# Reordering a sixteen-batch transformer-block kernel on all engines, with other places for the last batch's gate products and the first batch's loads

## What is computed

```python
def cross_attention(query, keys, values):            # 16 heads of 32, 120 keys per batch
    Q, K, V = query @ W_q.T, keys @ W_k.T, values @ W_v.T      # split into heads
    scores = Q K^T / sqrt(32) - slope[head] * (query_pos - key_pos)
    scores = where(mask == 0, -inf, scores)
    e = exp(scores - max(scores))
    return (e / (1 + sum(e))) V @ W_o.T
def ffn(x):                                          # x_prev: x moved by one token
    xr, xk = mu_r * x + (1 - mu_r) * x_prev, mu_k * x + (1 - mu_k) * x_prev
    return sigmoid(xr @ W_r.T) * (relu(xk @ W_k.T) ** 2 @ W_v.T)
x = x + tanh(g_xattn) * cross_attention(layernorm(x), ctx, ctx)
x = x + tanh(g_ffn) * ffn(layernorm(x))
```

## Time and profile before

| | before |
|---|---|
| median of 3 runs | 1311.96 us (1311.15 to 1312.66) |
| the profiled execution's own time | 1310.22 us |
| its span, first to last instruction | 1308.4 us |
| mean granted PE clock | 0.998 |
| busy PE / DVE / ACT / POOL | 1282.4 / 1068.7 / 837.4 / 786.9 us |
| mean DMA | 79 GB/s |

### The profile page before, as it was taken

How to read it: one execution, slowest core, us unless ns; L and a number is a source line. 1 busy time by engine, 2 the same in 40 slices (tenths; PEclk the granted TensorE clock), 3 DMA queues, 4 the chain that set the end, 5 groups by cost and what they waited for, 6 DMA issues and landing times.

```text
span 1308.4 us, 30826 instructions
## 1 busy us (share of the span) xinstructions
PE 1282.4 (98%) x9848; PEld 1044.2 (80%) x9848; DVE 1068.7 (82%) x2834; ACT 837.4 (64%) x2868; POOL 786.9 (60%) x731
## 2 busy tenths in 40 slices
PE   8999999999999999999999999999999999999998
PEld 7888778878777777877777787778778877878877
DVE  4667988888888888888888888888888888888864
ACT  5357483956758394765839486674839577584942
POOL 0015567676666667666666766666676766667641
PEclk9999999999999999999999999999999999999999
DMA  8762304031221304022120502222040412212000
GB/s 286 218 202 80 104 27 136 0 109 52 73 88 36 125 8 140 12 75 86 52 108 8 153 0 85 75 73 88 32 129 0 118 43 73 88 48 74 9 26 33
DMA packets 75377, 103.74 MB, mean 79 GB/s; under 512 B 26960, under 2 KB 33104, under 8 KB 75344
## 3 DMA queue, kind: packets, MB, share of 16 engines
q1 hardware_dynamic: 75344, 103.31, 25.2%
HBM read 78.62 MB, written 24.67 MB: 79 GB/s over the span
## 4 chain that ended last, share of the span: by engine, by line
PE 82%; DVE 6%; DMA 5%; issue 4%; POOL 2%; DVEq 0%; ACT 0%; POOLq 0%; SPq 0%
PE rotating L504 58%; PE score_bank L583 5%; PE probs_bank L677 4%; PE attn_bank L688 4%; PE attn_bank L677 4%; DMA rstd_row<-rstd_scratch 4%; PE score_bank L504 4%; PE score_bank L599 1%; DMA rstd_scratch<-rstd 1%; DVE norm L1221 1%; DVE mix_k L1231 1%; POOL rstd L1452 1%; DVE gated L1248 1%; DVE attn_t L1192 1%; PE probs_bank L599 1%
## 5 line engine op out<-in xcount | busy, mean ns | idle before, releaser
L877 ACT ACTIVATE probs<-probs,neg_max 128x120 f32<-128x120 f32 x1024 | 390.7, 388 | 3.6 <-DVE neg_max L1177 3.5
L1471 POOL TENSOR_TENSOR probs<-probs,recip 128x960 f32<-128x960 f32 x128 | 232.1, 1813 | 162.6 <-DVE recip L1188 162.6
L1173 DVE SCALAR_TENSOR_TENSOR probs<-mask_in,score_bank 128x120 f32<-128x120 f32 x1024 | 213.6, 270 | 27.6 <-PE score_bank L583 26.3
L504 PE MATMUL rotating<-w_proj,attn_t 128*128 128x512 f32 x768 | 192.9, 400 | 7.0 <-DVE attn_t L1192 7.0
L877 ACT ACTIVATION_READ_ACCUMULATOR probs<-probs,neg_max 128x1 f32 x1024 | 197.1, 192 | 0.0
L504 PE MATMUL rotating<-w_gate,mixed_gate 128*128 128x512 f32 x768 | 195.2, 400 | 1.2 <-DVE query_t L1158 1.1
L504 PE MATMUL rotating<-w_value,xt_or_act 128*128 128x512 f32 x720 | 180.8, 400 | 0.0
L504 PE MATMUL rotating<-mixed_key,w_key 128*128 128x512 f32 x720 | 178.7, 397 | 0.0
L504 PE MATMUL rotating<-xt_or_act,w_query 128*128 128x512 f32 x744 | 177.3, 394 | 0.0
L504 PEld LDWEIGHTS rotating<-w_proj,attn_t 128*128 128x128 f32 x768 | 140.8, 188 | 42.8 <-issue 12.5
L1177 DVE TENSOR_REDUCE neg_max<-probs 128x4 f32<-128x480 f32 x256 | 167.2, 653 | 8.8
(11 more groups left out here) (126 smaller groups left out, 2205.9 us busy)
## 6 DMA issues: line engine op xcount, KB each, us to landing
x_again<-in_x_dram SPq DMA_DIRECT2D x64, 256.0 KB, 2.7
xt_raw<-in_x_t_dram SPq DMA_DIRECT2D x16, 1024.0 KB, 8.0
xs<-in_x_dram SPq DMA_DIRECT2D x64, 256.0 KB, 5.4
out_dram<-gated SPq DMA_DIRECT2D x64, 256.0 KB, 2.0
rstd_row<-rstd_scratch SPq DMA_DIRECT2D x16, 256.0 KB, 5.3
value_scratch<-gated SPq DMA_DIRECT2D x16, 240.0 KB, 3.6
mask_in<-in_mask_dram SPq DMA_DIRECT2D x16, 240.0 KB, 2.9
keys_t<-key_scratch SPq DMA_DIRECT2D x16, 240.0 KB, 4.8
```

The source lines that it names most:

```text
L504: mm = pe.matmul(bank, stationary(a, c), moving(b, c), start=(i == 0), stop=(i == MATMULS - 1))
L877: e = act.activation(probs[:, t % 2, head, :], probs[:, t % 2, head, :], ACT.Exp, bias=neg_max[:, t % 2, head:head + 1], accum_out=sums[:, ...
L1173: z = dve.scalar_tensor_tensor(out=probs[:, t % 2, head, :], in0=neg_dist[:, t, :], scalar=SLOPES[head], in1=score_banks[j][:, g * NK:(g + ...
L1471: pool.tensor_tensor(part, part, recip[:, t % 2, heads].unsqueeze(2).to_broadcast((P, H // 2, NK)), ALU.mult)\
```

## The change

All five lists of the batch are put in another order; what each call does stays as it is, but for the splitting of `bias` on DVE into `bias_add` and `bias_max`, so that other work can stand between them. In the last batch, gate 0 and gate 1 are made ahead of `turn2(3)`, with other banks, and in the tail gate 2 and gate 3 stand each behind one half of the key products. On SP, loads and stores of the batch change places, and loads of the first batch (the x tiles for batch 1, weight 5) are issued at other points. `load_x` gets waits of its own, since it now stands ahead of stores whose waits it used to rely on.

```diff
 ATTENTION_AND_FFN = (
     ("gate", 0, -1), ("gate", 1, -1), ("key", 0, -1), ("key", 1, -1), ("key", 2, -1), ("key", 3, -1),
-    ("proj", 0, 0), ("value", 0, -1), ("value", 1, -1), ("proj", 1, 0), ("gate", 2, -1), ("value", 2, -1),
-    ("gate", 3, -1), ("proj", 2, 0), ("value", 3, -1), ("proj", 3, 0),
+    ("proj", 0, 0), ("value", 0, -1), ("value", 1, -1), ("gate", 2, -1), ("proj", 1, 0), ("value", 2, -1),
+    ("proj", 2, 0), ("gate", 3, -1), ("value", 3, -1), ("proj", 3, 0), ("query", 0, 1), ("query", 1, 1),
...
-        tail_bank = {("gate", t): rotating[t % 2] for t in range(QT)}
+        tail_bank = {("gate", t): bank for t, bank in enumerate((rotating[0], attn_bank, rotating[1], rotating[0]))}
...
             def load_x(b, t):
+                if earlier(b, 0, 2 * QT):
+                    sp.wait_ge(out_ready, (b - 2) * QT + t + 1)
...
             load_keys(0)
             load_values(0)
+            load_again(1, 0)
             store_chunk(4)
+            load_again(1, 1)
             for t in range(QT):
                 load_x(0, t)
-            load_weight(5)
...
                     load_xt(b + 1)
-                    load_again(b + 1, 0)
-                    load_again(b + 1, 1)
+                    load_weight(5)
...
                         load_again(b + 1, 0)
-                    for t in range(2):
-                        sp.wait_ge(out_ready, (b - 1) * QT + t + 1)
-                        store_out(b - 1, t)
+                        load_again(b + 1, 1)
+                        load_again(b + 1, 2)
+                    sp.wait_ge(out_ready, (b - 1) * QT + 1)
+                    store_out(b - 1, 0)
...
```

PE (between `turn_probs` 2,3 and the queries), and its tail:

```diff
-                use("proj", 1)
                 turn_probs(b, 2, 0)
                 turn_probs(b, 2, 1)
-                use("gate", 2)
+                use("gate", 2, range(9))
+                use("proj", 1)
                 turn_probs(b, 2, 2)
                 turn_probs(b, 2, 3)
+                use("gate", 2, range(9, MATMULS))
                 use("turn2", 0)
-                use("value", 2)
-                use("turn2", 1)
                 all_attends(2)
                 turn_probs(b, 3, 0)
-                use("gate", 3, range(6))
+                use("value", 2)
+                use("proj", 2)
                 turn_probs(b, 3, 1)
-                use("proj", 2)
+                use("turn2", 1)
                 turn_probs(b, 3, 2)
                 turn_probs(b, 3, 3)
-                use("gate", 3, range(6, MATMULS))
+                use("gate", 3)
                 all_attends(3)
+                use("turn2", 2)
                 use("value", 3)
                 use("proj", 3)
-                use("turn2", 2)
                 if last:
                     pe.wait_ge(read["value"], b * QT)
                     gate(b, 0, range(MATMULS), tail_bank).then_inc(done["gate"], 1)
+                    gate(b, 1, range(MATMULS), tail_bank).then_inc(done["gate"], 1)
                 use("query", 0)
                 use("query", 1)
+                use("query", 2)
                 use("turn2", 3)
-                use("query", 2)
                 use("query", 3)
...
-            pe.wait_ge(read["proj"], NB * QT)
-            tail("gate", 1)
...
-            for t in range(2, QT):
-                pe.wait_ge(read["gate"], f * QT + t - 1)
-                tail("gate", t)
+                if half == 0:
+                    pe.wait_ge(read["proj"], NB * QT)
+                else:
+                    pe.wait_ge(read["gate"], f * QT + 1)
+                tail("gate", 2 + half)
```

DVE (the second half of the batch, as it is after the change) and POOL:

```diff
+                bias(b, 3, 2)
+                bias(b, 3, 3)
+                reciprocals(b, 3, 0)
                 normalise2(b, 0)
...
                 residual(b, 1)
                 statistics2(b, 1)
+                after((distances_to_keys, None))
+                attn_low(b, 2)
+                mix_key(b, 0)
                 normalise2(b, 1)
+                reciprocals(b, 3, 1)
                 feed_forward((finish, 2))
+                residual(b, 2)
+                statistics2(b, 2)
                 after((statistics1, 3))
                 mix_gate(b, 0)
+                normalise2(b, 2)
                 mix_key(b, 1)
                 attn_low(b, 3)
                 mix_gate(b, 1)
                 feed_forward((finish, 3))
                 residual(b, 3)
                 statistics2(b, 3)
+                after((query_out, 0), (query_out, 1))
                 normalise2(b, 3)
...
```

```diff
                 normalise_probs(b, 3, 0)
                 edge(b, 0)
                 difference(b, 0)
+                rstd2_of(b, 1)
+                normalise_probs(b, 3, 1)
+                after((split_x_low, 1), (split_x_low, 2))
                 edge(b, 1)
-                normalise_probs(b, 3, 1)
+                rstd2_of(b, 2)
+                after((rstd1_of, None))
                 difference(b, 1)
-                rstd2_of(b, 2)
+                after((split_x_low, 3))
+                if last:
+                    mix_low(b, 0)
+                    mix_low(b, 1)
                 edge(b, 2)
...
```

More of the change, by code:

```diff
@@ L454, in batch @@
                         load_again(b + 1, 0)
-                    for t in range(2):
-                        sp.wait_ge(out_ready, (b - 1) * QT + t + 1)
-                        store_out(b - 1, t)
+                        load_again(b + 1, 1)
+                        load_again(b + 1, 2)
+                    sp.wait_ge(out_ready, (b - 1) * QT + 1)
+                    store_out(b - 1, 0)
                     if not last:
-                        for t in range(1, QT):
-                            load_again(b + 1, t)
+                        load_x(b + 1, 0)
+                    sp.wait_ge(out_ready, (b - 1) * QT + 2)
+                    store_out(b - 1, 1)
+                    if not last:
+                        load_again(b + 1, 3)
                         sp.wait_ge(scores_biased, (b + 1) * QT * G)
                         load_mask(b + 1)
-                        load_keys(b + 1)
-                        load_x(b + 1, 0)
                         load_x(b + 1, 1)
-                    if not last:
+                        load_x(b + 1, 2)
                         store_rstd(b + 1)
@@ L1160, in query_out, with bias_add @@
                                          op0=ALU.mult, op1=ALU.mult).then_inc(read["query"], 1)
-            def bias(b, t, g):
+            def bias_add(b, t, g):
                 if g == 0:
@@ L1178, in bias @@
                                   AX.X, ALU.max, negate=True).then_inc(max_ready, 1)
+            def bias(b, t, g):
+                bias_add(b, t, g)
+                bias_max(b, t, g)
             def reciprocals(b, t, half):
@@ L1308, in batch @@
                 bias(b, 0, 2)
+                reciprocals(b, 0, 0)
                 bias(b, 0, 3)
-                reciprocals(b, 0, 0)
-                bias(b, 1, 0)
+                after((statistics1, 0))
+                bias_add(b, 1, 0)
+                reciprocals(b, 0, 1)
+                bias_max(b, 1, 0)
                 bias(b, 1, 1)
-                reciprocals(b, 0, 1)
                 bias(b, 1, 2)
@@ L1316, in batch @@
                 reciprocals(b, 1, 0)
+                after((statistics1, 1))
                 bias(b, 2, 0)
-                bias(b, 2, 1)
+                bias_add(b, 2, 1)
                 attn_low(b, 0)
-                bias(b, 2, 2)
+                bias_max(b, 2, 1)
+                bias_add(b, 2, 2)
                 reciprocals(b, 1, 1)
+                bias_max(b, 2, 2)
                 bias(b, 2, 3)
+                after((statistics1, 2))
                 residual(b, 0)
+                bias(b, 3, 0)
                 statistics2(b, 0)
-                after((statistics1, 0))
-                bias(b, 3, 0)
                 bias(b, 3, 1)
@@ L1330, in batch @@
                 attn_low(b, 1)
+                feed_forward((finish, 1))
+                reciprocals(b, 2, 1)
                 bias(b, 3, 2)
+                bias(b, 3, 3)
+                reciprocals(b, 3, 0)
                 normalise2(b, 0)
-                reciprocals(b, 2, 1)
-                feed_forward((finish, 1))
-                reciprocals(b, 3, 0)
                 residual(b, 1)
                 statistics2(b, 1)
-                bias(b, 3, 3)
+                after((distances_to_keys, None))
+                attn_low(b, 2)
+                mix_key(b, 0)
                 normalise2(b, 1)
-                after((statistics1, 1), (statistics1, 2))
+                reciprocals(b, 3, 1)
                 feed_forward((finish, 2))
-                attn_low(b, 2)
-                reciprocals(b, 3, 1)
+                residual(b, 2)
+                statistics2(b, 2)
                 after((statistics1, 3))
-                residual(b, 2)
-                mix_key(b, 0)
-                statistics2(b, 2)
                 mix_gate(b, 0)
+                normalise2(b, 2)
                 mix_key(b, 1)
@@ L1355, in batch @@
```

(3 more changed lines are left out.)

113 lines of the change are left out of this document (61 added, 52 removed).

## The result

| | before | after |
|---|---|---|
| median of the runs | 1312.31 us | 1287.49 us (1286.61 to 1287.98) |
| ratio, 95% interval | | 0.9815 (0.9801 to 0.9829) |
| profiled execution, its span | 1310.22, 1308.4 us | 1286.61, 1284.8 us |
| busy PE / DVE | 1282.4 / 1068.7 us | 1271.9 / 1048.6 us |
| length of a batch | 75.05 us | 73.63 us |

(The median of before is that of the runs made beside it.) The change makes the kernel 24.8 us faster, 1.9%. The forecast was 1292 us, the range 1282 to 1306.

The account below looks back on a forecast made before the run. PE's own work, busy 98%, was taken as the bound. Span 1308.4 - 15.4 (loop) - 0.8 (first batch) - 3.8 (tail) = 1288.4 us; 1290.2 us profiled, 1292 us for the runs; range 1282 to 1306.

Parts of the forecast that it names:

- Loop: Batches after the first: 75.05 us each falling to 73.95 us, 15.4 us gained over 14 batches.
- The walk through the queues: PE's order set out from gate 0 (T = 0), other engines laid beside it, to find new waits; next gate 0 at 73.5.
- two tight places: turn2(2) at T = 56.1 and proj 3 at 59.4, without slack; new waits of 0.2 us a batch for both.
- scores beside attends: Scores 2 directly ahead of attends 0 saves one slow change between kinds of matmul: half of 0.20 us taken, 0.10 a batch.
- part 1: Proj 1 on PE: two groups of transposes and nine gate 2 matmuls in front remove its wait, 0.75 us a batch.
- part 2: turn2(3) behind query 2 on PE, 2.73 us later: its wait goes, 0.29 plus 0.16 us a batch.
- First batch: Wait ahead of turn2(2) may stay in part, query_out 2's is not touched: 0.8 us gained, bounds 0.5 lost and 2.5 gained.
- Tail: Last batch's end: idle ahead of turn2(3) and slow clock go, 1.0 us idle at gate 2 stays; 3.8 us gained, bounds 2 and 4.9.
- SP: Moved loads and stores on SP cost nothing; without cover, a load of 3 to 6 us once per batch.
- R1: POOL's rstd1_of power holds DVE's normalise2(2); turn2(2) waits 1.15 us a batch, 13.3 us less gain, 1305 us; chance 0.14.
- R2: POOL's holds of DVE between attn_low 2 and attn_low 3 delay proj 3: 2.8 us new waits a batch, 1328 us; chance 0.12.

Follow-up runs that it names:

- difference 1 between: Changed kernel with difference 1 between the addition and the power of the 512 scales (rstd1_of) on POOL: 1284.49 us, ratio 0.9802; once more, 1284.21 us.
- difference 1 first: Changed kernel with difference 1 ahead of rstd1_of, the making of the scales, on POOL: 1289.75 us, ratio 0.9839.
- the reduction added: Changed kernel with one unused reduction of 128x512 elements on DVE ahead of the second layer norm of tile 2: 1285.47 us, ratio 0.9809.

## Why the prediction was right, and where it was not

**Loop.** Forecast 73.95 us a batch, measured 73.63; 15.4 us against 19.0 (18.5 and batch 1's 0.5). The walk through the queues held at its two tight places: norm 2 was to end at T = 55.5 and ended at 723.92 - 668.5 = 55.4; attention 3's low part at 59.25 and 59.1. Elsewhere not all of it held: norm 0 ended at 709.85 - 668.5 = 41.4 where I had 41.9, and `attn_low` 2 ended at 46.4 as forecast although its parts did not (the mask came after 0.34 us and not 0.7, and the `distances_to_keys` behind it took 1.71 us where they had taken 0.88 before). New waits were to be 0.2 us a batch and are 0.17. The terms that were too small: scores beside attends, half of 0.20 taken, all of it measured (0.23 in the run that parts them); and one wait of before that I did not count, `turn2(0)`, 0.60 us in the chain of before where 0.44 is four transposes (by the trace it waited for the last `bias` of tile 3, which ended 0.1 us before). These give 0.10 + 0.16 + 0.03 = 0.29 us; part 2 takes 0.06 from it, so that of the 0.32 us some 0.1 stays open.

```profile
721.83 0.60 PE score_bank L599 x4
```

**The step that failed in its reason** is part 1: I gave the 0.75 us at proj 1 to the gate matmuls put in front of it. With these taken away proj 1 does not wait either (0.2 us once in the whole span). The other moves are enough to remove its wait, through `finish` 0, which takes 0.93 us instead of 1.46; which of them does it, on DVE, POOL or PE, was not tested one by one. The gates in front are needed for something that I did not name, ACT's queue of `probs_out` and exponentials; without them the kernel is slower than before (75.83 us a batch). That the size came out was luck in part: the old wait is gone either way, and its size was read from the trace of before; what the move I named is worth, 2.2 us a batch, I had wrong by a factor of three.

**Layer norm of tile 3** (part 2): 0.45 forecast, 0.39 measured on its own. The price of an idle time was too high there: 0.6 us for 0.45, not 0.7.

**First batch.** 0.8 us forecast, within bounds of 0.5 lost and 2.5 gained; measured 0. The 1.2 us ahead of `turn2(2)` went, but the wait for `query_out` 2 grew from 1.10 to 2.46 us: I had said that it was not touched. It is counted from the end of the queries, and these now end earlier, while the split of weight 5 took 3.12 us where it had taken 2.27 in the trace of before. `query_out` 2 starts at 151.12 in both.

```profile
146.13 2.27 DVE L1117 TENSOR_TENSOR w_value<-xs,w_value 128x2048 fp32r<-128x2048 f32 x1
```

```profile
145.85 3.12 DVE L1132 TENSOR_TENSOR w_value<-xs,w_value 128x2048 fp32r<-128x2048 f32 x1
```

**Tail.** 3.8 us forecast, 4.55 in the traces, 4.1 by the undone tail. Gate 2 waited 0.73 us where I had 1.0, and a key half takes 1266.96 - 1261.20 = 5.76 us where I had 5.9; the values begin 1269.70 - 1245.88 = 23.8 us after proj 3 and not 24.7. No lower clock, as forecast.

**SP.** I took its moves at nothing. No run undoes them; PE waits for no DMA in any of these traces, and in the changed kernel's batch `query_out` 0 waits for PE (0.83 us) and no longer for the scales' load (0.45 us before).

**Rivals.** R1 falls for the power and holds for a full-size operation; in the changed kernel only the small one stands beside that norm. R2 (holds that add up between `attn_low` 2 and 3) did not occur: there was one hold of 0.87 us (`finish` 2, 1.62 us), and norm 2 behind it ended on time all the same. A rival that I did not have, a wait on ACT, was the one that decides here whether proj 1 may stand in front.

## What to carry to other kernels

With one engine 98% busy, an order can still be worth 2%: set its work out by the pitch of its pieces, lay the other queues beside it and compare at each wait; that walk was good to 0.2 us here at the two places without slack, and up to 0.5 us off elsewhere. Give a removed wait to an edit only after undoing that edit alone, since a move on one engine may be there for a queue on another. Operations of full size that hold each other, here norms, `finish` and splits on DVE against differences, scalings and low parts on POOL, should not become ready at the same time; a small operation ahead of the large one settles who goes first.

## What the runs showed of the hardware that I had not expected

Between kernels that do the same at the end of the first batch, PE idled 2.46 to 2.54 us there, and its granted clock fell behind it in some traces and not in others. It stayed at 1.00 in both traces of the changed kernel (2.46 and 2.50), the one with proj 1 back (2.46), the one with scores and attends apart (2.52) and the first of the one with difference 1 between (2.54); it fell in the one with difference 1 first (2.52; two stretches of 2 us):

```profile
152.00:154.00 2.00, 2.00 (x10) 1.17 (x13) 2.00 (x4) 0.00 (x0) 1.73 (x2) 0.73 1.00 332
154.00:156.00 2.00, 2.00 (x33) 1.79 (x30) 1.81 (x7) 1.26 (x3) 0.09 (x1) 0.50 0.97 330
```

From gate 0 to the same piece of the next batch it then took 229.88 - 151.78 = 78.10 us instead of 76.89, 1.0 us more beside the 0.17 of its longer batch. It also fell with the old tail (2.49), with the reduction added (2.48), and in the second trace of the kernel with difference 1 between (2.52; 0.63 and 0.51 in the same two stretches), so that one and the same kernel did both: from gate 0 to the piece behind it took 228.94 - 151.29 = 77.65 us in its second trace and 228.18 - 151.58 = 76.60 in its first. The two traces are of different chips, but on one chip the changed kernel kept its clock (2.50) and this one lost it (2.52), so the chip does not decide it; what does is not shown. So the same idle time costs 1 us more or not from trace to trace, and single spans of these kernels are only good to about that; the length of a batch is the better measure: by the same equal pieces it was 73.63 us in both traces of the changed kernel (the second: (1186.68 - 229.44) / 13), and 73.44 and 73.41 us in those of the one with difference 1 between (the second: (1183.23 - 228.94) / 13).
